# A histogram of source blocks counted by planes of digit values on two engines, with extra matmuls beside it

## The reference

```
h  = maximum(layernorm(x), 0)
e  = silu(concat([h[src], h[dst], edge_weight1]) @ eW1 + eb1)
e  = silu(e @ eW2 + eb2)
agg = segment_sum(e, src, num_segments=12500)
out = x + silu(concat([h, agg]) @ nW1 + nb1) @ nW2 + nb2
```

## Time and profile before

| what | value |
|---|---|
| median of 3 runs | 4410.79 us (4405.56 to 4414.93) |
| the profiled execution | 4406.18 us, of which the span of its instructions 4404.4 us |
| busy share of the span: PE, DVE, ACT, POOL | 71%, 52%, 44%, 53% |
| mean granted TensorE clock | 0.864 of full |
| sources and destinations in SBUF | 17.8 us |
| histogram: first comparison to reading of the counts | 22.0 to 92.0 us |
| small steps up to the first onehot | 92.0 to 100.5 us |
| first ranks | 110.8 us |

### The profile page before, as it was taken

One profiled execution on the slowest core, in us unless ns is written; L12 is line 12 of the kernel. 1 busy time (PEld: TensorE's weight loads), 2 busy tenths in 40 slices (PEclk: granted clock), 3 DMA queues, 4 the chain that ended last, 5 costly groups with the idle time before them and its releaser, 6 DMA issues.

```text
span 4404.4 us, 87094 instructions
## 1 busy us (share of the span) xinstructions
PE 3137.3 (71%) x24183; PEld 2716.0 (62%) x24184; DVE 2308.7 (52%) x7968; ACT 1934.7 (44%) x4269; POOL 2323.8 (53%) x2362
## 2 busy tenths in 40 slices
PE   5788888888756666666666666666666666666668
PEld 4476777766656666666666665666666566656664
DVE  8678787777644444444444444444444444444441
ACT  0478788787733333333333333333333333333331
POOL 0144444444565565555555555555655555565540
PEclk9788888788788888888888888888888888888889
DMA  2000000000011111111111111111111111111784
GB/s 67 9 17 19 15 20 15 19 15 19 10 43 41 42 42 41 42 41 41 42 42 41 41 42 41 41 42 42 41 41 41 42 41 42 42 41 41 40 44 79
DMA packets 379595, 161.56 MB, mean 37 GB/s; under 512 B 324822, under 2 KB 347670, under 8 KB 379478
## 3 DMA queue, kind: packets, MB, share of 16 engines
q0 software_dynamic: 75008, 126.93, 13.5%
q1 hardware_dynamic: 304310, 32.32, 5.9%
q10 hardware_dynamic: 160, 0.85, 0.1%
HBM read 139.38 MB, written 20.53 MB: 36 GB/s over the span
## 4 chain that ended last, share of the span: by engine, by line
another core or an unknown queue 39%; PE 36%; ACT 9%; DVE 8%; issue 6%; SPq 1%; DMA 0%; POOL 0%; ACTq 0%; DVEq 0%; POOLq 0%
PE bk L892 10%; ACT ED L1058 6%; PE bk L811 6%; PE bk L890 4%; PE bk L882 3%; PE bk L797 2%; PE bk L799 2%; PE bk L798 1%; PE bk L843 1%; DVE GA L512 1%; PE bk L880 1%; DVE BIG L541 1%; DVE P L446 1%; PE bk L793 1%
## 5 line engine op out<-in xcount | busy, mean ns | idle before, releaser
L372 POOL DMA_INDIRECT GA<-q_d,RB x1876 | 1822.4, 971 | 1248.2 <-remote 693.4
L699 DVE TENSOR_TENSOR BIG<-bk,BIG 128x128 f32 x1876 | 547.6, 292 | 1651.1 <-remote 875.3
L1058 ACT ACTIVATE ED<-bk,eb1c 128x512 f32<-128x512 f32 x469 | 322.3, 687 | 1617.1 <-remote 1473.7
L890 PE MATMUL bk<-B,ones 128*128 128x512 bf16 x469 | 202.8, 432 | 946.6 <-ACT ED L1058 942.9
L359 POOL DMA_INDIRECT rec_d<-BIG,GA x468 | 492.8, 1053 | 704.7 <-ACT BIG L993 378.4
L882 PE MATMUL bk<-OHS,P 128*128 128x128 bf16 x5628 | 685.7, 247 | 0.0
L890 PEld LDWEIGHTS bk<-B,ones 128*128 128x128 bf16 x469 | 45.9, 98 | 1030.4 <-ACT ED L1058 792.6
L892 PEld LDWEIGHTS bk<-W,ED 128*128 128x128 f32 x3752 | 604.9, 230 | 18.6
L880 PE MATMUL bk<-identf,GA 128*128 128x128 f32 x1876 | 604.8, 322 | 12.4 <-issue 7.7
L882 PEld LDWEIGHTS bk<-OHS,P 128*128 x5628 | 575.7, 115 | 54.1
L892 PE MATMUL bk<-W,ED 128*128 128x128 f32 x3752 | 609.0, 316 | 0.0
(11 more groups left out here) (182 smaller groups left out, 3203.6 us busy)
## 6 DMA issues: line engine op xcount, KB each, us to landing
GA<-q_d,RB POOLq DMA_INDIRECT x1876
RB<-rec_d SPq DMA_DIRECT2D x469, 8.0 KB
rec_d<-BIG,GA POOLq DMA_INDIRECT x468
q_d<-QS SPq DMA_DIRECT2D x14, 448.0 KB
rec_d<-ED SPq DMA_DIRECT2D x16, 236.0 KB, 10.7
hT_d<-HT SPq DMA_DIRECT2D x14, 224.0 KB
P<-hT_d SPq DMA_DIRECT2D x8, 384.0 KB, 9.9
P<-in_x SPq DMA_DIRECT2D x8, 384.0 KB, 9.3
```

Source lines behind the costliest of these rows:

```text
L372: e.indirect_dma_start(G[k * U + u], None, q_d, bass.IndirectOffsetOnAxis(ap=RB[k][:, u, 1:2], axis=0))\
L699: e.tensor_tensor(AGG[:, ds(v, P)], banks[6 + k % 2][:, u * P:(u + 1) * P], AGG[:, ds(v, P)], ALU.add).then_inc(s["ad"], 1)
L890: e.matmul(z[:, :], ones[:, :], B2[:, :, :].rearrange("p a b -> p (a b)"), start=True, stop=False)
L1058: e.activation(E1[k % 2], banks[2 + k % 2][:, :], ACT.Silu, bias=eb1c[:, :]).then_inc(s["e1"], 1)
```

## The change

The comparisons are made per value of the digit. For a quarter of the columns (QC = 416, 13 groups, 4 quarters) GpSimd writes 8 planes of `OA`, one `tensor_scalar` each against a constant, with a step of 8 elements, and VectorE writes 16 planes of `OB`, which is now laid out with the 416 columns innermost. Both have two buffers; quarter q + 2 waits until TensorE has used quarter q (`f1`). TensorE counts a quarter (`tally`, 13 groups of 8 matmuls), whose moving operand now takes the 16 low digits with a step of 416 elements. ScalarE copies the two banks to SBUF (`sums`), TensorE picks the parts with equal column by four fp32 matmuls against `PICK` (`pick`), ScalarE copies 8 rows by 208 (`cnt`), and at the end 16 fp32 matmuls against `SPREAD` put the counts of all groups into bank 2. VectorE's masks and folds go; it makes `PICK`, `BOFF` and `SPREAD` before the edges have come. `BK`, `VAL` and the first seven onehots are made by VectorE before it waits for the counts, not behind. TensorE gets 32 extra matmuls of 512 columns ahead of the histogram (WARM) and one extra in each of the first 18 steps of the main loop, into a bank that nobody reads.

```diff
+            e.wait_ge(s["hl"], 1)
+            for q in range(NQC):
+                ge(e, s["f1"], q - 1)
+                for b in range(8):
+                    ins = e.tensor_scalar(OA[q % 2][:, :, b], HI[:, q * QC:(q + 1) * QC], float(b), None, ALU.is_equal)
+                ins.then_inc(s["oa"], 1)
...
-            def counts(r):
-
-                e.wait_ge(s["f1"], 2 * r + 2)
-                link(e.tensor_tensor(M1, banks[r % 2][0:32, 0:256].rearrange("p (s j l) -> p s j l", j=4, l=16),
-                                     MK.rearrange("p (s j) l -> p s j l", s=1).broadcast_to([32, 4, 4, 16]), ALU.mult))
-                link(e.tensor_reduce(RR, M1.rearrange("p s j l -> p s l j"), axis=AX.X, op=ALU.add))
...
+            for q in range(NQC):
+                ge(e, s["f1"], q - 1)
+                for b in range(16):
+                    ins = e.tensor_scalar(OB[q % 2][:, b, :], LO[:, q * QC:(q + 1) * QC], float(b), None, ALU.is_equal)
                 ins.then_inc(s["o1"], 1)
...
+            for b in range(LEAD // 2):
+                onehot(b)
+
+            e.wait_ge(s["hc"], 1)
...
+            e.wait_ge(s["pk"], 1)
+            for k in range(WARM):
+                e.matmul(banks[7][:, :], ones[:, :],
+                         ones[:, :].rearrange("p (a b) -> p a b", a=1).broadcast_to([P, 4, P]), start=True, stop=True)
+
+            def tally(q):
+
+                e.wait_ge(s["o1"], q + 1)
+                e.wait_ge(s["oa"], q + 1)
+                ge(e, s["sm"], 2 * (q - 1))
+                for r in range(QS_):
+                    z = banks[q % 2 * 5 + r // 8][0:32, r % 8 * 64:r % 8 * 64 + 64]
+                    for m in range(8):
+                        c = SC * r + m * 4
+                        last = e.matmul(z, OA[q % 2][:, c:c + 4, :].rearrange("p c h -> p (c h)"),
+                                        OB[q % 2][:, :, c:c + 4].rearrange("p l c -> p c l"),
+                                        start=(m == 0), stop=(m == 7))
+                last.then_inc(s["f1"], 1)
+
+            def pick(q):
+
+                e.wait_ge(s["sm"], 2 * q + 2)
+                ge(e, s["cs"], q)
+                v = SUMS[q % 2].rearrange("p (s j l) -> p s j l", j=4, l=16)
+                for j in range(4):
+                    last = e.matmul(banks[4][0:8, 0:QS_ * 16], PICK[:, j, :], v[:, :, j, :],
+                                    start=(j == 0), stop=(j == 3))
+                last.then_inc(s["rr"], 1)
...
+            e.wait_ge(s["cs"], NQC)
+            for l in range(16):
+                last = e.matmul(banks[2][:, 0:NS], SPREAD[:, l, :], CNT[:, :, l], start=(l == 0), stop=(l == 15))
+            last.then_inc(s["hc"], 1)
...
+                if t < OFF:
+                    e.matmul(banks[7][:, :], ones[:, :],
+                             ones[:, :].rearrange("p (a b) -> p a b", a=1).broadcast_to([P, 4, P]),
+                             start=True, stop=True)
...
+            def sums(q):
+
+                e.wait_ge(s["f1"], q + 1)
+                ge(e, s["rr"], q - 1)
+                for a, b, n in ((0, 0, 512), (512, 1, QS_ * 64 - 512)):
+                    e.activation(SUMS[q % 2][:, a:a + n], banks[q % 2 * 5 + b][0:32, 0:n], ACT.Copy).then_inc(s["sm"], 1)
```

More of the change, by code:

```diff
@@ L114, in gnn @@
         TWv = P3all[:, 0:2 * C].bitcast(fp32)
-        CG = 64
+        NQC = 4
+        QC = C // NQC
+        QS_ = NS // NQC
         HI, LO = (P3all[:, a * C:(a + 1) * C] for a in (2, 3))
         o1 = 4 * C
[L118 to L126, removed]
+        PLN = [P3all[:, o1 + j * 24 * QC:o1 + (j + 1) * 24 * QC] for j in range(2)]
+        OA = [t[:, 0:8 * QC].rearrange("p (c h) -> p c h", h=8) for t in PLN]
+        OB = [t[:, 8 * QC:].rearrange("p (l c) -> p l c", c=QC) for t in PLN]
+        o1 += 48 * QC
+        SUMS = [P3all[0:32, o1 + j * QS_ * 128:o1 + (j + 1) * QS_ * 128].bitcast(fp32) for j in range(2)]
+        o1 += QS_ * 256
+        CNT = P3all[0:8, o1:o1 + NS * 32].bitcast(fp32).rearrange("p (s l) -> p s l", l=16)
+        o1 += NS * 32
+        SPREAD = P3all[0:8, o1:o1 + 4096].bitcast(fp32).rearrange("p (l b) -> p l b", b=P)
+        o1 += 4096
+        PICK = P3all[0:32, o1:o1 + 64].bitcast(fp32).rearrange("p (j h) -> p j h", h=8)
+        o1 += 64
+        BOFF = P3all[0:8, o1:o1 + 2 * P].bitcast(fp32)
+        o1 += 2 * P
+        PICKC = P3all[0:32, o1:o1 + 8].bitcast(fp32)
+        PICKH = P3all[0:32, o1 + 8:o1 + 24].bitcast(fp32)
+        assert o1 + 24 <= 3 * NPAD
         BT = sb("BT", [1, NT], i32)
@@ L231, in gnn @@
         LEAD = 14
+        WARM = 32
         def node_steps(parts):
@@ L450, in _ @@
                 ins.then_inc(s["o1"], 1)
-                if g and g % 2 == 0:
-                    counts(g // 2 - 1)
-            counts(NS // 4 - 1)
             link(e.tensor_single_scalar(T32, SRC, 7, op=ALU.arith_shift_right))
             link(e.tensor_copy(BK[:, :], T32))
-            e.wait_ge(s["hc"], NS)
+            link(e.tensor_scalar(T32, SRC, P - 1, 14, ALU.bitwise_and, ALU.logical_shift_left))
+            link(e.tensor_tensor(T32, T32, DST, ALU.add))
+            link(e.tensor_scalar(VAL[:, :, 0:1], T32.rearrange("p (c w) -> p c w", w=1), 16384.0, None, ALU.add))
@@ new lines, in _, with onehot @@
+            iota_b = iob[:, 0:NBIN].rearrange("p (a w) -> p a w", a=1).broadcast_to([P, 8, NBIN])
+            def onehot(b):
+                i, r, u = batch(b)
+                c = (2 * i + r // 2) * SC + r % 2 * HC + u
+                bk = BK[:, c:c + 8].rearrange("p (c w) -> p c w", w=1).broadcast_to([P, 8, NBIN])
+                e.tensor_tensor(OH[i % 2][:, r, u:u + 8, :], iota_b, bk, ALU.is_equal).then_inc(s["o2"], 1)
+            for b in range(LEAD // 2):
+                onehot(b)
+            e.wait_ge(s["hc"], 1)
@@ L629, in _ @@
             link_m = {}
[L630 to L635, removed]
             for t in range(NR + OFF + 3):
@@ L748, in _ @@
             e.wait_ge(s["cm"], 1)
[L749 to L769, removed]
@@ new lines, in pick @@
+            def pick(q):
[6 more added lines that the diff above has]
+                last.then_inc(s["rr"], 1)
+            for q in range(NQC):
+                tally(q)
+                if q:
+                    pick(q - 1)
@@ L1033, in _, with cnt @@
             e.activation(VAL[:, :, 1:2], TWv.rearrange("p (c w) -> p c w", w=1), ACT.Copy).then_inc(s["vw"], 1)
+            def sums(q):
[3 more added lines that the diff above has]
+                    e.activation(SUMS[q % 2][:, a:a + n], banks[q % 2 * 5 + b][0:32, 0:n], ACT.Copy).then_inc(s["sm"], 1)
+            def cnt(q):
+                e.wait_ge(s["rr"], q + 1)
+                e.activation(CNT[:, q * QS_:(q + 1) * QS_, :].rearrange("p s l -> p (s l)"), banks[4][0:8, 0:QS_ * 16],
+                             ACT.Copy).then_inc(s["cs"], 1)
+            for q in range(NQC):
+                sums(q)
+                if q:
+                    cnt(q - 1)
+            cnt(NQC - 1)
             base(0)
```

38 lines of the change are left out of this document (13 added, 25 removed).

## The result

The change makes the kernel slower: 4446.51 us as the median of 4 runs (4439.47 to 4452.28) against 4408.18 of the kernel before on the same chip (4 runs), a ratio of 1.0082 with a 95% interval of 1.0065 to 1.0099. That is 38 us more by the medians, 29 to 44 us by the interval. The forecast was 4378.

A forecast was written before the change was run, and what follows sets the result against it. VectorE was taken to bound the histogram, and no engine the whole kernel. From 4406.2 us, 25 saved before the first ranks and 3 by TensorE's clock gave 4378, range 4358 to 4404.

The forecast's parts named there:

- t = 0.7: Histogram: time in us of one GpSimd compare of 128x416, the middle between 0.37 and 0.96; 32 such compares.
- the formula of two for one: Histogram: two VectorE compares get in between two GpSimd compares; counts at 48.6+32t, 71 us in the forecast.
- that of one for one: Histogram: one VectorE compare gets in between two GpSimd compares; counts at 54.9+32t, 77 us in the forecast.
- The engines' exclusion: Histogram: a VectorE compare waits out a GpSimd instruction; VectorE compares near 0.8 us beside GpSimd, mostly 0.2 when it is idle.
- the moved steps: BK, VAL and seven onehots before the counts' wait: hidden by ScalarE's and TensorE's tail; up to 12 us if uncovered.
- The tally: Histogram: TensorE's 104 matmuls for a quarter take 6.0 us, the first one starting at 31 to 36 us.
- My second rival: Tally's stepped read halves the rate: 11.1 us each, TensorE bounds, 4394 us; chance 0.16 shared with t of 1.0 to 1.6.
- The tail: After the last tally: ScalarE copies, four fp32 matmuls, small copy, 16 fp32 matmuls (4 us); 9 us with hand-overs.
- From the counts to the first ranks: VectorE's steps after the counts (7.0 us), then the first ladder step (4.8): 11.8 us, first ranks at 85.8.
- The extras: First ladder steps: extra matmuls raise TensorE's clock, gaining 8 us if it holds, nothing if not; 3 us taken.
- The slow rival: Histogram: GpSimd's compares become the bound, break-even at t = 1.38, 4423 us at 2 us a compare; chance 0.10.
- my three signs of being wrong: GpSimd compares over 1 us; tallies of 10 us; later stages (4293.6 us after the first ranks) changing by over 10 us.

The follow-up runs named there:

- p1: Kernel before plus unread GpSimd and VectorE compares of several forms ahead of the histogram, alone and together; 3750.11 us in one execution, including the added work.
- p2: Kernel before plus six tallies on filler data (contiguous, stepped, runs of four), each alone and behind 24 large matmuls; 3802.9 us in one execution, including the added work.
- e3: Changed kernel with the tally's moving operand read in runs of four neighbouring columns; 4431.65 us (one execution) against 4411.80 for the kernel before.
- e4: Kernel before with only BK, VAL and the first seven onehots moved ahead of the wait for the counts; 4416.22 us against 4411.80, ratio 1.0008.
- e1: Changed kernel without both sets of extra matmuls; 3692.01 us against 3656.58 for the kernel before on that chip, ratio 1.0098.
- e6: Kernel of e5 plus three extra matmuls in each of the first 18 ladder steps; 4366.63 us against 4411.80 for the kernel before, ratio 0.9888.
- e5: Changed kernel without GpSimd compares or extras: VectorE compares 416x8 contiguously per quarter, tally reads runs of four; 4366.14 us against 4411.80 for kernel before, ratio 0.9899.
- e8: Kernel of e6 again on another chip; 3630.72 us against 3664.96 for the kernel before, ratio 0.9907.

## Why the prediction was wrong, point by point

**What bounds the kernel.** Right: the first 150 us are a chain, and a difference at the first ranks goes to the end one for one. 38.9 us there are 38.7 at the end in the changed kernel.

**GpSimd's compares: the step that failed.** The forecast took t = 0.7 from a MEMSET at 0.89 ns an element and a two-level IOTA at 2.3. Measured: 2.91. Of that, 1.27 from start to start is a contiguous pass of 416 on GpSimd (p1), above my upper end. Neither of my rows had a read in it: a MEMSET of 416 fp32, which only writes, took 0.52 us in p1 against the compare's 1.25. The step of 8 in the write adds 1.4, and VectorE's work beside it 0.3. I had called that step "never shown" and still taken the middle. This one term is worth 2.2 times 32 = 71 us, more than the distance from 74 to 139.

That GpSimd, once it is the bound, costs 32t was right. With t = 2.91 the formula of two for one gives 48.6+93.1 = 141.7 for the counts, that of one for one 148, and they came at 138.77; but the nearness of the first is in part luck. It has 33.5 us ahead of the 32t (19.9, 2.1 and VectorE's 11.5), where 20.2 were measured, because GpSimd did not wait for VectorE's compares in turn (what it lost to them, 0.3 a compare, is in t); and it has 15 behind (tally 6, tail 9), where 25.4 were measured. The two errors, 13 too much and 10 too little, nearly cancel.

The Trainium skill's cycles for a comparing loop (GPSIMD Engine Reference, Performance pitfalls for Q7 kernels: 1.03 to 2.03 an element) would be, as an estimate with that page's 1.2 GHz, 0.36 to 0.70 us for 416; the run disagrees, 1.25 contiguous. The Trainium skill's general word on that page (Performance versus the Vector engine), that VectorE is the engine for elementwise work, was the rule to go by. Its factor of about two is given for an operation with two inputs; for this compare with one input p1 measured 6.6 (1.25 to 0.19, both contiguous).

**The engines' exclusion.** That an engine waits out an instruction of the other is seen again, mostly on VectorE, whose compares took 0.74 us on average in the changed kernel and 0.19 alone; but VectorE was not the bound, so it mattered little. GpSimd's compares became 10% longer beside VectorE's (2.64 to 2.91), and more where VectorE ran its long 32-bit steps. These are GpSimd's eight compares for the third quarter (65.8 to 87.6 us, VectorE idle for half of that time) and its eight for the fourth (87.7 to 113.2, beside BK, VAL and the onehots), each from the groups of its stretch:

```profile
L369 POOL TENSOR_SCALAR P<-P 128x416 bf16<-128x416 bf16 x8 | 21.6, 2857 | 0.3
```

```profile
L369 POOL TENSOR_SCALAR P<-P 128x416 bf16<-128x416 bf16 x8 | 25.3, 3316 | 0.3
```

So the moved steps, which I had at nothing under cover, seem to have lengthened the cover itself by 3.7 us; no run without them in this place tells for certain. More than two VectorE compares came in between two of GpSimd's: VectorE did 32 while GpSimd did its first 8, 2.9 us each.

**VectorE's compares.** Right for VectorE alone: 0.18 taken, 0.19 measured in p1.

**The tally.** 6.0 taken, 11.62 measured. My second rival had the size (11.1) and the cause, the stepped read, but worked it out in cycles of 1.2 GHz; p2 shows its matmuls just as slow at the higher clock, so that part of the agreement is luck. Hidden behind GpSimd but for the last, the slow read cost 6.5 us (e3), not the 15.5 of that rival, in which TensorE is the bound.

**The tail.** 9 taken, 13.8 measured. Missed: the `pick` of the third quarter stands behind the last tally in TensorE's queue (2.9 and not beside anything), and the 16 matmuls against SPREAD took 7.1 and not 4. That is 0.22 us a pass, with the clock at 0.50; my bounds, 3.4 to 6.4, came from line 811's passes at the two clocks, and I took a value near the lower. Line 752 of the kernel before, whose weights are 128 wide too, takes 1.86 us for 8 passes, 0.23 each; I passed that row over.

**From the counts to the first ranks.** 11.8 taken, 10.9 measured (11.2 in e4, in the same order). With the moved steps, that is 8 us less than the 18.8 before. Right in mechanism; but by e4 the move alone loses 3.5, and its gain is there only while VectorE has time to spare.

**The extras.** 3 taken, 0.8 to 0.9 measured in the first 16 steps (against e1 and against the kernel before), and no more than the noise at the end (1.0082 with, 1.0098 without): the clock read 0.54 of full in the ladder steps with one extra, 1.00 with three (e6).

**The slow rival** was the right one: t as the bound, price 32t, break-even at 1.38. At 0.10 its chance was too low. It rested on a form (a stepped write, arithmetic on GpSimd) of which the trace has no row at all. Such a gap, in a term that counts 32 times, deserves a range well above the dearest row (0.96); here the term came out at three times that row. Two of my three signs of being wrong came true, compares over 1 us and tallies over 10; the third did not, as the later stages took 4293.4 us for 4293.6.

## What to carry to other kernels

A compare of bf16 values against a constant is nearly free on VectorE when it writes side by side (0.19 us for 416), and five to fourteen times as dear when it writes with a step or is given to GpSimd; before planes are split over engines, price one plane of that very form on that engine. GpSimd with a contiguous write was not run in the kernel; by an estimate from p1's 1.41 us beside VectorE its 32 compares would take 45 us, where VectorE makes all planes of e5 in 25.5. When the reader needs another order than the writer, let each have runs: four neighbours were enough for TensorE to read at full rate. And steps moved ahead of a wait only gain if their engine is idle there (e4: 3.5 us lost without that).

## What the runs showed of the hardware that I had not expected

- GpSimd, 416 elements, one input: 1.25 us for bf16 and fp32, is_equal and multiply alike; with a write step of 16 bytes 2.76 us.
- VectorE, 416 bf16 elements against a constant: 0.19 us contiguous, 0.94 with the same step.
- TensorE, moving operand of 64 bf16 columns: 112 ns a matmul with a step of 832 bytes between columns, at 1.2 and at 2.4 GHz alike (p2); 31 ns in runs of four at the higher clock (3.23 us for 104).
- 104 such matmuls without a gap, in stepped order, took 11.62 us in p2 whatever came before; the contiguous ones took 5.16 us from an idle start and 3.21 behind large matmuls.
- The first of the three matmuls of 396 columns in a ladder step took 0.33 to 0.35 us at the higher clock and 0.49 to 0.51 at the lower. The lower clock came from step t = 3 on without extras (e1, e5), with one extra matmul of 512 columns in each step from t = 4 in the changed kernel but from t = 10 in e3, and with three in none of the steps t = 1 to 15 (e6, e8). Why one extra did so much more in e3 stays open.
